# Gated cross-attention and mixture of experts on one core: the second batch's context prepared during the first batch's attention, and the last tile's gating computed from x_new

## The reference, cut to what matters

```python
q1 = fake_quant(layernorm(x), ...); q2 = fake_quant(ctx, ...)       # round, clip to 0..255, rescale
x = x + tanh(g_xattn) * matmul(q1, q2)                              # per batch: (512, 1024) @ (1024, 1024)
y = layernorm(x)
logits = y @ W_gate + b_gate; top_idx = top_k(logits, 2)
y_all = relu(einsum(y, W_e) + b_e)                                  # 8 experts, 1024 x 1024 each
x = x + tanh(g_ffn) * mean of y_all over the two chosen experts
```

## Time and profile before

| | |
|---|---|
| profiled execution | 366.18 us |
| its span, first to last instruction | 364.4 us |
| mean granted TensorE clock | 0.966 |
| TensorE busy, matmuls | 323.4 us, 89% |
| VectorE busy | 229.5 us, 63% |
| ScalarE busy | 133.7 us, 37% |
| GpSimd busy | 112.5 us, 31% |

### The profile page before, as it was taken

The page is one execution under the profiler, slowest core; times in us unless marked ns, Lnnn a source line. Parts: engine busy times, 40 slices in busy tenths (PEclk is TensorE's granted clock), DMA queues, the critical chain, the costliest instruction groups (busy, mean ns, idle before and its releaser), DMA issues.

```text
span 364.4 us, 7003 instructions
## 1 busy us (share of the span) xinstructions
PE 323.4 (89%) x1732; PEld 251.3 (69%) x1740; DVE 229.5 (63%) x361; ACT 133.7 (37%) x113; POOL 112.5 (31%) x131
## 2 busy tenths in 40 slices
PE   0579787998877999999999999999999999999960
PEld 0224364677844888888888888888888888888840
DVE  2898998886987973298949434933239434943220
ACT  3865876544503621267335114401135114411100
POOL 3552445000012314154128333233314332333310
PEclk9999999999569999999999999999999999999995
DMA  6999577320595997499998974995239943454233
GB/s 229 414 409 385 182 298 304 149 98 19 206 333 179 412 402 161 112 296 376 362 358 224 400 162 122 335 341 117 38 115 310 353 109 114 114 115 103 38 89 58
DMA packets 23004, 81.46 MB, mean 224 GB/s; under 512 B 3152, under 2 KB 3152, under 8 KB 22992
## 3 DMA queue, kind: packets, MB, share of 16 engines
q1 hardware_dynamic: 16656, 58.76, 42.0%
q0 software_dynamic: 6192, 22.55, 25.8%
q10 hardware_dynamic: 144, 0.01, 0.0%
HBM read 62.43 MB, written 18.87 MB: 223 GB/s over the span
## 4 chain that ended last, share of the span: by engine, by line
PE 73%; DVE 16%; DMA 3%; issue 3%; POOL 1%; ACT 1%; POOLq 0%; DVEq 0%; ACTq 0%
PE ps L1214 60%; PE ps_y L1190 5%; PE ps L1021 4%; DVE st L698 4%; DVE xt L762 2%; DMA y_rows<-y_scratch,idx 2%; DMA par<-in_small_dram 2%; PE ps_s L1073 1%; DVE onehot L823 1%; PE ps_y L1048 1%; PE ps L1028 1%; DVE mv L700 1%; DVE lnv L720 1%; DVE u8c L744 1%; POOL q L408 1%
## 5 line engine op out<-in xcount | busy, mean ns | idle before, releaser
L1214 PE MATMUL ps<-w_hi,yT_hi 128*128 x320 | 126.5, 395 | 0.5 <-DVE yT_lo L950 0.5
L1214 PE MATMUL ps<-w_hi,yT_lo 128*128 x320 | 124.8, 390 | 0.0
L1214 PE MATMUL ps<-w_lo,yT_hi 128*128 x320 | 124.5, 389 | 0.0
L829 DVE TENSOR_TENSOR w_lo<-stage,w_hi 128x2048 f32 (+1 forms) x32 | 72.0, 2286 | 11.3 <-ACT w_hi L633 9.6
L482 POOL DMA_INDIRECT out_dram<-res,sidx x20 | 32.7, 1634 | 133.9 <-DVE res L984 119.0
L633 ACT ACTIVATE w_hi<-stage 128x2048 f32 x28 | 52.5, 1911 | 57.1 <-PE ps L1214 37.8
L981 DVE TENSOR_TENSOR res<-ps,bias 128x512 f32<-128x512 f32 x40 | 27.5, 688 | 67.8 <-issue 36.2
L1214 PEld LDWEIGHTS ps<-w_hi,yT_hi 128*128 128x128 f32 x320 | 60.1, 188 | 12.7 <-issue 0.9
L1214 PEld LDWEIGHTS ps<-w_hi,yT_lo 128*128 128x128 f32 x320 | 60.1, 188 | 12.7
L1214 PEld LDWEIGHTS ps<-w_lo,yT_hi 128*128 128x128 f32 x320 | 60.2, 188 | 11.8
L620 ACT ACTIVATE yT_hi<-ps_y 128x1024 fp32r<-128x1024 f32 x21 | 21.4, 1021 | 114.4 <-PE ps_y L1190 114.4
(11 more groups left out here) (156 smaller groups left out, 261.6 us busy)
## 6 DMA issues: line engine op xcount, KB each, us to landing
stage<-in_L_ffn_W_e_dram SPq DMA_DIRECT2D x32, 1024.0 KB, 7.5
stage<-in_ctx_dram SPq DMA_DIRECT2D x16, 512.0 KB, 11.7
xt<-in_x_dram SPq DMA_DIRECT2D x8, 512.0 KB, 11.4
y_scratch<-y SPq DMA_DIRECT2D x8, 512.0 KB, 3.0
out_dram<-xt SPq DMA_DIRECT2D x8, 512.0 KB, 3.1
bias<-in_L_ffn_b_e_dram SPq DMA_DIRECT2D x8, 512.0 KB, 4.3
y_rows<-y_scratch,gidx POOLq DMA_INDIRECT x22, 5.5
out_dram<-res,sidx POOLq DMA_INDIRECT x20, 6.3
```

What stands on the lines that cost most here:

```text
L829: dve.tensor_tensor(w_lo[:, dst], stage[:, CK * c:CK * (c + 1), :].rearrange("p k h -> p (k h)"), w_hi[:, dst].bitcast(f32), ALU.subtract) ...
L1214: last = pe.matmul(ps[q][:, h * 512:(h + 1) * 512], lhs[q][:, k, :], w[:, bass.ds(woff + k * D + h * 512, 512)], start=(k == 0 and lhs is ...
```

## The change

- The second batch's contexts are quantised earlier on ScalarE, 9 before q1T(2), and 10 to 15 with fewer steps between them. GpSimd centres q1(4) and q1(5), which VectorE did, between contexts 12, 13 and 14.
- The second batch's column sums go into `ps_y` too, and stand on TensorE in pieces: context 8 before attention(2), 9 to 11 before attention(3), 12 and 13 and transpose_q1(4) inside it, 14 and 15 after it. `transpose_y(0)` waits until they are read out.
- On VectorE, `read_rowsums(0)` and `keep_colsum_lo(1)` move up to before stats(1,2); the centring of q1(4) and q1(5) goes. On ScalarE std(1,0) and normalise(1) move behind keep_q1T(4), keep_q1T(5) behind keep_yT(1). On TensorE transpose_q1(5), transpose_y(1) and gate(0) move behind fold(4).
- The last tile: y(7) is made by ScalarE, before keep_yT(7). `transpose_y(7)` transposes x_new(7) itself and doesn't wait for y(7). The logits of that tile are corrected afterwards: A times the gate sums plus B times the column total of W_gate plus the bias. The total comes from three small additions on GpSimd (`wpart`) and one matmul with ones (`gate_sums`); two small operations on VectorE apply it (`shift`).
- There are two groups, 0 to 3 and 4 to 7: the third select, counts, positions and slot matrix go.

```diff
-        gates_in = (ps_s[:, NT:NT + TPB * E], ps_g[:, 0:TPB * E], ps[0][:, 0:E])
-        GROUPS = ((0, TPB), (TPB, NT - 1), (NT - 1, NT))
+        gates_in = (ps_s[:, NT:NT + TPB * E], ps_g[:, 0:TPB * E])
+        wsum_in = ps_g[:, TPB * E:(TPB + 1) * E]
+        GROUPS = ((0, TPB), (TPB, NT))
...
-        POOL_Q1, DVE_Q1 = (0, 1, 2, 6), (3, 4, 5, 7)
-        ACT_Y, DVE_Y = (1, 2), (0, 3, 4, 5, 6, 7)
+        POOL_Q1, DVE_Q1 = (0, 1, 2, 4, 5, 6), (3, 7)
+        ACT_Y, DVE_Y = (1, 2, 7), (0, 3, 4, 5, 6)
...
+            pool.memset(ones_f[:, :], 1.0)
...
-            for k in range(KT + 1, 2 * KT):
+            for k in range(KT + 1, KT + 5):
                 centre_ctx(k)
+            centre_q1(4)
+            centre_ctx(KT + 5)
+            centre_q1(5)
+            centre_ctx(KT + 6)
+            centre_ctx(KT + 7)
             pool.wait_ge(s_att, TPB)
             pool.iota(iota_pe[:, :, :], [[1, P], [0, E]], base=0, channel_multiplier=0,
+            pool.wait_ge(s_wg, 16)
+            pool.tensor_tensor(wpart[:, 0:4, :], wg[:, 0:4, :], wg[:, 4:8, :], ALU.add).then_inc(s_wt, 1)
+            pool.wait_ge(s_wt, 1)
+            pool.tensor_tensor(wpart[:, 4:6, :], wpart[:, 0:2, :], wpart[:, 2:4, :], ALU.add).then_inc(s_wt, 1)
+            pool.wait_ge(s_wt, 2)
+            pool.tensor_tensor(wpart[:, 6, :], wpart[:, 4, :], wpart[:, 5, :], ALU.add).then_inc(s_wt, 1)
...
             quantise_ctx(8)
+            quantise_ctx(9)
             keep_q1T(2)
             keep_colsum_hi(0)
-            quantise_ctx(9)
+            quantise_ctx(10)
             std(0, 4, 2, 3)
-            quantise_ctx(10)
+            quantise_ctx(11)
+            quantise_ctx(12)
+            keep_q1T(3)
             quantise_x(4)
-            quantise_ctx(11)
-            keep_q1T(3)
-            quantise_ctx(12)
+            quantise_ctx(13)
             quantise_x(5)
-            quantise_ctx(13)
-            std(1, 0, 2, 1)
             quantise_ctx(14)
-            normalise(1)
             quantise_ctx(15)
             keep_q1T(4)
+            std(1, 0, 2, 1)
+            normalise(1)
+            keep_colsum_hi(1)
             keep_yT(0)
-            keep_q1T(5)
             std(1, 2, 2, 2)
             keep_yT(1)
-            keep_colsum_hi(1)
+            keep_q1T(5)
             normalise(2)
...
             std(1, 7, 1, 6)
+            normalise(7)
             keep_yT(7)
...
+                m = n - 1 if e == NT else n
+                if e == NT:
+                    link(dve.scalar_tensor_tensor(shift[:, :], wsum_in, lnv[:, 1, BB, NT - 1:NT], bg, ALU.mult, ALU.add))
+                    dve.scalar_tensor_tensor(lg[:, m, :], gates_in[g][:, m * E:n * E], lnv[:, 1, AA, NT - 1:NT],
+                                             shift[:, :], ALU.mult, ALU.add)
...
             stats(1, 0, 0)
-            centre_q1(4)
             stats(1, 1, 1)
...
             x_new(3)
-            centre_q1(5)
+            read_rowsums(0)
+            keep_colsum_lo(1)
             stats(1, 2, 0)
             stats(1, 3, 2)
             x_stats(7)
-            read_rowsums(0)
             scales(1, 2, 2, 2)
             normalise(3)
             scales(0, 6, 2, 4)
-            keep_colsum_lo(1)
             x_new(4)
...
             scales(1, 7, 1, 6)
-            normalise(7)
             positions(0)
             slot_matrix(0)
-            select(1)
-            read_rowsums(1)
             dve.wait_ge(s_iota, 1)
             for i in range(TPB):
                 make_onehot(i)
+            select(1)
+            read_rowsums(1)
             positions(1)
             slot_matrix(1)
-            select(2)
-            for i in range(TPB, NT - 1):
+            for i in range(TPB, NT):
                 make_onehot(i)
-            positions(2)
-            slot_matrix(2)
-            make_onehot(NT - 1)
...
+            def gate_sums():
+                pe.wait_ge(s_wt, 3)
+                pe.matmul(wsum_in, ones_f[:, :], wpart[:, KT - 2, :], start=True, stop=True)
...
-            for i in (2, 3):
-                attend_after(i)
-                attend_half(i, 0)
-                attend_half(i, 1)
-                fold(i)
-            pe.wait_ge(s_xn, 3)
-            column_sums(KT, KT + 4)
-            transpose_q1(4)
-            transpose_y(0)
-            column_sums(KT + 4, KT + 6)
-            transpose_q1(5)
-            transpose_y(1)
+            column_sums(KT, KT + 1)
+            attend_after(2)
+            attend_half(2, 0)
+            attend_half(2, 1)
+            fold(2)
+            column_sums(KT + 1, KT + 4)
+            attend_after(3)
+            attend_half(3, 0)
+            column_sums(KT + 4, KT + 6)
+            transpose_q1(4)
+            attend_half(3, 1)
+            fold(3)
             column_sums(KT + 6, 2 * KT)
-            pe.wait_ge(s_qe, 6)
             rowsums(0)
             attend_after(4)
             attend_half(4, 0)
-            gate(0)
+            transpose_y(0)
             attend_half(4, 1)
             fold(4)
+            pe.wait_ge(s_rs, 1)
+            transpose_q1(5)
+            transpose_y(1)
+            gate(0)
             transpose_y(2)
...
             counts(0)
+            transpose_y(7)
+            gate_sums()
             gate(6)
-            transpose_y(7)
-            pe.wait_ge(s_xn, NT - 1)
+            gate(7)
+            pe.wait_ge(s_xn, NT)
             rowsums(1)
-            counts(1)
-            gate(7)
...
             place_rows(0)
-            counts(2)
+            counts(1)
             place_rows(1)
-            place_rows(2)
```

More of the change, by code:

```diff
@@ L90, in flamingo_gated_moe @@
         tri = at("tri", [P, E + 1, E], f32, YT + 10 * KB + 256)
+        ones_f = at("ones_f", [P, P], f32, WLO + 8 * KB)
+        wpart = at("wpart", [P, KT - 1, E], f32, WLO + 9 * KB)
         iota_pe = at("iota_pe", [P, P, E], bf16, WLO + 32 * KB)
@@ L116, in flamingo_gated_moe @@
         lg = sb("lg", [P, TPB, E], f32)
+        shift = sb("shift", [P, E], f32)
         rank = sb("rank", [P, TPB, E], f32)
@@ L197, in flamingo_gated_moe @@
         s_gate = sem("gating_in_psum")
+        s_wt = sem("gate_sum_step")
         s_lg = sem("logits_read")
@@ L263, in slab @@
         def slab(i):
-            return i % 2 if i < TPB else (i + 1) % 2
+            return i % 2
         def slots(eng, body):
@@ L518, in keep_colsum_hi @@
                 act.wait_ge(s_cp, b + 1)
-                act.activation(cs[:, b, :], (ps_k if b == 0 else ps[0])[:, :], ACT.Copy).then_inc(s_csh, 1)
+                act.activation(cs[:, b, :], ps_k, ACT.Copy).then_inc(s_csh, 1)
             def normalise(i):
-                act.wait_ge(s_ab[1], i // 2 + 1)
+                act.wait_ge(s_ab[1], 6 if i == NT - 1 else i // 2 + 1)
                 if i >= 2:
@@ L691, in keep_colsum_lo @@
                 dve.wait_ge(s_csh, b + 1)
-                dve.tensor_tensor(cs[32:64, b, :], (ps_k if b == 0 else ps[0])[32:64, :], cs[32:64, b, :],
+                dve.tensor_tensor(cs[32:64, b, :], ps_k[32:64, :], cs[32:64, b, :],
                                   ALU.subtract).then_inc(s_cs, 1)
@@ L779, in select @@
                 dve.wait_ge(s_gate, e)
-                dve.tensor_tensor(u(lg), gates_in[g][:, 0:n * E].rearrange("p (i e) -> p i e", e=E),
-                                  bg.unsqueeze(1).to_broadcast([P, n, E]), ALU.add).then_inc(s_lg, 1)
+                m = n - 1 if e == NT else n
[3 more added lines that the diff above has]
+                                             shift[:, :], ALU.mult, ALU.add)
+                dve.tensor_tensor(lg[:, 0:m, :], gates_in[g][:, 0:m * E].rearrange("p (i e) -> p i e", e=E),
+                                  bg.unsqueeze(1).to_broadcast([P, m, E]), ALU.add).then_inc(s_lg, 1)
                 dve.wait_ge(s_lg, g + 1)
@@ L1009, in column_sum @@
             def column_sum(k):
-                into = ps_k if k < KT else ps[0]
                 for h in range(HB):
-                    last = pe.matmul(into[:, h * 512:(h + 1) * 512], ones_b[:, :], q2[:, k, h * 512:(h + 1) * 512],
+                    last = pe.matmul(ps_k[:, h * 512:(h + 1) * 512], ones_b[:, :], q2[:, k, h * 512:(h + 1) * 512],
                                      start=(k % KT == 0), stop=(k % KT == KT - 1))
@@ L1032, in attend_after @@
             def attend_after(i):
[L1033 to L1036, removed]
+                pe.wait_ge(s_xn, i - 1)
                 pe.wait_ge(s_qe, i + 1)
@@ L1043, in transpose_y @@
             def transpose_y(i):
-                wait_y(pe, i)
+                if i == NT - 1:
+                    pe.wait_ge(s_xn, NT)
+                else:
+                    wait_y(pe, i)
                 if i >= 1:
                     pe.wait_ge(s_ye, i)
+                else:
+                    pe.wait_ge(s_cs, 2)
+                rows = xt[:, i, :] if i == NT - 1 else y[i % 2][:, :]
                 for k in range(KT):
```

(11 more changed lines are left out.)

## The result

The changed kernel takes 371.42 us (median of 4 runs, 369.81 to 372.24), the one before 365.89 on the same chip (4 runs): ratio 1.014 [1.011, 1.017]. Forecast were 363.3, with a range up to 366.4, and "faster" as the likeliest. The profiled execution took 372.21 (span 370.5) against 366.18 (364.4): +6.1 us of span to explain.

What follows compares the result with a forecast made beforehand. TensorE's unchanged 248.5 us expert walk, whose start hangs on the index list: read at 101.25 + 0.3 = 101.55 against 104.82, −3.3. From 366.18 that gives 362.9, plus 0.33 and rounded up 363.3; range 361.6 to 366.4.

Steps and rivals of the forecast that it cites:

- I take +0, its own row: First gather, after the index list: keeps its 5.75 despite later stores, biases and weights; ends −1.3 to +3.0.
- an estimate of 1.3 more: First gather: sharing DMA engines in turn with stores and weights would add some 1.3 us, giving 364.6.
- 83.7 for x_new(7): End of the middle stretch: x_new(7) starts at 83.7 instead of 85.06, gain 1.35.
- 46.6 for x_new(3): Middle stretch on VectorE: x_new(3) comes at 46.6, against 46.53 before, reached through scales(1,0) and normalise(0).
- the moved additions: GpSimd's three additions for the column total: 0 to 3.3 in all, delaying only two stores not awaited before 104; taken as 0.
- Rival 3: Hole at 54.4 to 56.4 before gate(0): clock falls, attention(5) and gate(1) cost 3.5 + 1.7 more, 368.4; chance 0.13.
- the weight split: Middle, VectorE: first weights' split ends at 67.2; fold(5) no longer late, so x_new(5) follows directly, gain 0.35.
- One selection round less: Tail: select, counts, positions and slots for a single tile go; tokens read at 101.25 before the clock's +0.3.
- normalise(7) off VectorE: Tail after x_new(7): VectorE's normalise(7), 0.73, leaves the chain.
- where I took +0.3: Clock at gate(7) in the tail: only the last of gate(7) slow, +0.3; ends 0 and +2.6.
- The column total on TensorE: Before gate(7): fp32 matmul of 0.12 to 1.9, hidden up to there by 0.8 free on TensorE; taken as 0.
- The two small operations: VectorE in the tail, applying the correction to the logits: 0.3 to 2.0, taken as 0.4.

Runs made afterwards that it cites:

- e3: The changed kernel with the second batch's row sums made before the gate sums and read ahead of positions(0): 366.24 us, 0.999 of the kernel before.
- e4: The kernel before with only read_rowsums(1) moved from behind select(1) to behind select(2): 370.74 us, ratio 1.010.
- e5: The changed kernel with SyncE sending biases and next weights only after the first gather has landed: 368.83 us, 1.006 of the kernel before.
- e6: e3 with GpSimd's iota and three additions moved behind add_rowsum(1): 364.92 us, 0.996 of the kernel before.
- e2: The kernel before with only the tail of the change, the middle as before: 371.32 us, ratio 1.011.
- e7: The changed kernel with 46 filler matmuls in place of 20 ahead of the first gather's transposes: 370.54 us, 1.011 of the kernel before.
- e9: e8 without the six filler matmuls around gate(6): 363.55 us, 0.992 of the kernel before.
- e11: e9 without the eight filler matmuls in TensorE's hole ahead of gate(0): 364.72 us, 0.995 of the kernel before.
- e8: The changed kernel with rowsums(1) between gates (6) and (7), read before select(1), late iota, eight fillers before gate(0), six around gate(6): 364.02 us, 0.993 of before.
- e1: The kernel before with only the middle part of the change, the tail as before: 367.03 us, ratio 1.003.
- e10: e9 with GpSimd's add_rowsum(2) waiting until VectorE's centre_q1(7) is done: 363.65 us, 0.991 of the kernel before.

## Why the prediction was wrong

**The failed step is the gather, "I take +0, its own row".** It named the right mechanism ("sends four stores, two biases and the next weights 1.7 later") and then priced it from rows in which those loads were already done or nearly so the earlier trace rows. What decides isn't how long gathers take elsewhere, but how much SyncE has issued around this one and not yet moved. Before, the next weights were issued 4.8 ahead of the gather (101.64 to 106.44); the forecast itself made that 3 less for the earlier gather and 1.7 less for the later read, so nothing. That subtraction was there to be made. It measured +4.75, outside my −1.3 to +3.0, and 1.77 came on top since the wait outlasted the fillers; for this the prediction had no term. Together 6.5 of the 9.4 us between the span that the forecast implies (364.4 − 3.3 = 361.1) and the measured one (370.5). e3, e4 and e5 show it from three sides.

The traces hold a better price than the duration of a gather. Count its landing from the issue of the first of the four stores: 16.1 us in the kernel before (96.08 to 112.19), 15.5 in the changed one (101.02 to 116.55), and 13.8 to 17.2 in all ten kernels in which the gather was issued within 12 us of that store and the loads weren't held back, whether it was issued 4.6 or 11.4 behind it. With the loads held back (e5) it was 9.6. So this landing moves with the stores and hardly with the index list. With before's 16.1 and the prediction's own "1.7 later" the gather would have landed 1.7 later than before, not 3.3 earlier: an estimate of 368.3 where the forecast says 363.3. In e3 and e6, issued 13.8 and 13.2 behind that store, the gather met a nearly empty queue and took 4.5 and 4.6.

By the rule of the Trainium skill (DMA: Bandwidth & Descriptors, section "Queues, rings and completion order") that each DMA engine serves its queues in turn, I had an estimate of 1.3 more. It had the right sign, and I left it out of the sum. The measurement is more than three times as much. The queue rows show turns only late: 53.8% and 47.0% from 112 to 114, but q0 has no packet from 107.25 to 110 and 15.9% from 110 to 112. It began when about as much had moved as was issued ahead of it: 3.1 MB in the changed kernel, 2.7 to 2.9 in e2, e4 and e7, 2.1 (the stores) in e5. Why it begins only then stays open.

**The middle: 2.3 of the rest.** Predicted 83.7 for x_new(7), measured 85.98. The first of it is one operation. The new program lets GpSimd reach the iota at 46.01, 0.05 ahead of VectorE's normalise(0) at 46.06, and that takes 2.43, not 0.81. My 46.6 for x_new(3) became 48.41, and every later handover carried 1.5 to 2.3 of it: gate(0) 58.22 (56.4), x_new(4) 61.03 (59.4), x_new(5) 68.72 (67.2), x_new(6) 76.09 (74.1). I had costed the moved additions by where GpSimd's *results* were needed, not by what they run beside. The Trainium skill (SBUF — State Buffer, section "SBUF: two separate sides") says that VectorE in a mode with two ports and GpSimd share a pair of ports that whoever starts first holds for the whole instruction. The trace agrees in the main: the iota ends at 47.95 and normalise(0) 0.54 later, though behind a complete block one would expect its whole 0.81. In the kernel before GpSimd had reached the iota at 49.39, beside statistics. That rule, held against the moved iota, would have warned of the step. With the iota late and the hole filled the middle is what I worked out: x_new(3) 46.7, x_new(7) 83.3 in e9.

**Rival 3 happened in its place and not in its size.** The hole (56.15 to 58.22, then the eight-column gate) was found, and the clock fell near 60, later than the "before 58.3" from which I let it decide, and was back by 64. It cost some 1.1 at x_new(7) where only the fillers differ (e11 against e9), not 3.5 + 1.7. e7 has the early iota and no fall near 60, and x_new(6) at 75.41, where the changed kernel has 76.09 and the forecast 74.1: there 1.3 is without the fall and 0.7 goes with it. At x_new(7) the 2.3 can't be split like that, since e7's clock fell later (0.50 from 82 to 84). The fall near 60 isn't the change's alone: e2 and e4, with the old middle, had a fall there as well in the executions profiled, while the profile of before had none. x_new(5) did follow the weight split, as predicted. e6 and e11 are the same program up to x_new(7) and reached it at 85.95 and 84.41, e8 and e9 too, at 84.89 and 83.30: one trace of this stretch is uncertain by some 1.6, so the 1.1 leans on the medians' 1.2.

**Right.** One selection round less, and normalise(7) off VectorE: tail 18.44 (predicted 17.85, before 19.76). Gate(7) was all at half clock (3.58: +1.7 where I took +0.3, within its ends); part came back as its input was ready 0.4 sooner after x_new(7). The column total on TensorE took 0.29 and was hidden. The two small operations took 0.4. The expert walk is unchanged. As numbers: 2.3 middle, 0.6 tail, 4.75 gather, 1.77 clock: 9.4. These are stretches of one chain and not independent prices, since the middle and the tail also make the stores late.

With its three side effects removed the change gives about what was forecast for it: e9 is 2.8 us under before by ratio, against 3.3 forecast. I had predicted the change as if it had none.

## What to carry to other kernels

Before moving an operation behind another on one engine, list what other engines issue once it's done, and when the queue they feed must be empty again; price a latency-critical gather by the bytes still waiting ahead of it and issued just behind it, not by the duration of its quiet siblings. When an operation of GpSimd moves, look at which VectorE operation it will now lie beside. And where a wait grows, check that the fillers still cover it, without outlasting it.

## Not expected of the hardware

- A gather of 0.5 MB took 4.5 to 6.9 us when the weights had been issued 4.6 or more ahead of it or were held back, and 8.8 to 11.31 when biases and weights were issued within 1.6 us on either side of it (the changed kernel, e2, e4, e7). Within the first group it is 5.75, 4.92, 4.99, 6.05 and 6.89 at nearly the same distance (4.7 to 4.9: before, e1, e9, e11, e10); what sets that spread stays open.
- VectorE's f32 normalise took 0.81, and 2.43 beside a GpSimd iota of 1.94; a conversion 0.69, and 1.56 beside GpSimd's additions. Batch-norm statistics beside the same iota, in the kernel before, kept their 1.29 for two.
- In e9 TensorE was busy for all of 84 to 94: its last transposes ended at 86.9, and gates of eight columns and row sums of one followed. The granted clock was 1.00 to 88, 0.53 from 88 to 90 and 0.50 from 90 to 94: the profile can show TensorE fully busy at half its clock.
